# Two half-width feed-forward turns at the start of a decoder layer, with a new order of work

## The reference

```
x = x + linear_attention(layernorm(x))        # elu+1 feature map, causal sums, q k v and output projections
x = x + softmax_attention(layernorm(x), ctx)  # queries from x, keys and values from ctx, no output projection
x = x + feed_forward(layernorm(x))
feed_forward:
    h = silu((x @ w1.T) * s1) * ((x @ w2.T) * s2)     # 256 -> 1024
    h = gelu((h @ h1.T) * sh1)                        # 1024 -> 1024
    h = gelu((h @ h2.T) * sh2)                        # 1024 -> 1024
    return (h @ w3.T) * s3                            # 1024 -> 256
```

## Time and profile before

| | |
|---|---|
| median of 3 runs | 1086.01 us |
| the profiled execution | 1086.11 us, span 1084.3 us |
| PE busy | 1052.5 us, 97% of the span |
| DVE busy | 760.0 us, 70% |
| ACT busy | 554.6 us, 51% |
| POOL busy | 260.1 us, 24% |
| moved by DMA | 165.42 MB, mean 153 GB/s |

### The profile page before, as it was taken

One profiled execution on the slowest core, in us unless ns is written; L12 is line 12 of the kernel. 1 busy time (PEld: TensorE's weight loads), 2 busy tenths in 40 slices (PEclk: granted clock), 3 DMA queues, 4 the chain that ended last, 5 costly groups with the idle time before them and its releaser, 6 DMA issues.

```text
span 1084.3 us, 25055 instructions
## 1 busy us (share of the span) xinstructions
PE 1052.5 (97%) x9898; PEld 875.7 (81%) x9898; DVE 760.0 (70%) x1708; ACT 554.6 (51%) x871; POOL 260.1 (24%) x363
## 2 busy tenths in 40 slices
PE   6998899999999999999999999999999999999997
PEld 6897678787888878878878888788887888887886
DVE  5988987778777888868998767986589626423421
ACT  4344364654646455666454755465634663433431
POOL 3232351012410152011522111611027001500500
PEclk9999899999999999999999999999999999999999
DMA  4468677435633355243442325433254445555542
GB/s 132 151 207 288 212 236 240 131 106 181 195 109 132 121 190 177 79 151 116 172 148 89 118 72 187 129 117 110 100 177 123 135 136 181 187 187 171 179 156 72
DMA packets 72614, 165.42 MB, mean 153 GB/s; under 512 B 9904, under 2 KB 25392, under 8 KB 72496
## 3 DMA queue, kind: packets, MB, share of 16 engines
q1 hardware_dynamic: 69040, 152.26, 43.4%
q10 hardware_dynamic: 3456, 11.54, 3.4%
HBM read 140.66 MB, written 34.64 MB: 162 GB/s over the span
## 4 chain that ended last, share of the span: by engine, by line
PE 80%; DVE 10%; DMA 3%; issue 2%; POOL 2%; ACT 1%; SPq 1%; ACTq 0%; DVEq 0%; POOLq 0%
PE bank L1220 40%; PE bank L1105 7%; PE bank L1205 7%; PE bank L1240 5%; PE bank L1078 5%; PE bank L1047 4%; PE bank L1062 3%; PE bank L1052 2%; PE bank L1023 2%; DMA ctx_in<-in_ctxT 1%; PE bank L1155 1%; DVE mx L954 1%; DVE hidden_full L985 1%; DVE att_l L933 1%; DMA weight_ring<-weights_scratch 1%
## 5 line engine op out<-in xcount | busy, mean ns | idle before, releaser
L1220 PE MATMUL bank<-hidden_a,weight_ring 128*128 128x512 f32 x1024 | 251.9, 396 | 0.0
L1220 PE MATMUL bank<-hidden_b,weight_ring 128*128 128x512 f32 x1024 | 247.1, 394 | 0.3 <-DVE inexact_flag L1010 0.3
L1220 PEld LDWEIGHTS bank<-hidden_b,weight_ring 128*128 128x128 f32 x1024 | 188.2, 188 | 40.1 <-issue 1.2
L1220 PEld LDWEIGHTS bank<-hidden_a,weight_ring 128*128 128x128 f32 x1024 | 186.9, 188 | 39.5 <-issue 0.6
L822 ACT ACTIVATE hidden_full<-bank,columns_sb 128x512 f32<-128x512 f32 x128 | 88.2, 689 | 169.6 <-PE bank L1220 169.1
L671 POOL TENSOR_TENSOR ve<-mv,eps 128x1 f32<-128x1 f32 (+1 forms) x80 | 19.9, 249 | 491.9 <-DVE mv L837 491.9
L1205 PE MATMUL bank<-hidden_b,weight_ring 128*128 128x512 f32 x512 | 123.7, 396 | 1.3 <-DMA weight_ring<-weights_scratch 1.3
L1205 PEld LDWEIGHTS bank<-hidden_b,weight_ring 128*128 128x128 f32 x512 | 95.4, 190 | 22.5 <-DMA weight_ring<-weights_scratch 2.1
L710 POOL TENSOR_TENSOR hidden_a<-hidden_full,hidden_a 128x512 fp32r<-128x512 f32 x64 | 83.2, 1304 | 125.3 <-ACT hidden_a L817 123.8
L874 DVE STREAM_TRANSPOSE by_token<-bank 128x512 f32<-128x512 f32 x64 | 45.5, 711 | 87.7 <-PE bank L1078 87.6
L993 DVE TENSOR_TENSOR hidden_a<-hidden_full,hidden_a 128x512 fp32r<-128x512 f32 x64 | 44.0, 692 | 68.3 <-ACT hidden_a L828 68.1
(11 more groups left out here) (135 smaller groups left out, 1727.6 us busy)
## 6 DMA issues: line engine op xcount, KB each, us to landing
weight_ring<-weights_scratch SPq DMA_DIRECT2D x160, 512.0 KB, 3.7
weights_scratch<-in_h ACTq DMA_DIRECT2D x16, 512.0 KB, 5.5
xn3T_scratch<-hidden_b SPq DMA_DIRECT2D x16, 512.0 KB, 3.8
weight_bits<-in_h SPq DMA_DIRECT2D x32, 256.0 KB, 3.9
weight_ring<-weights_scratch SPq DMA_DIRECT2D x32, 256.0 KB, 2.8
x_in<-in_x SPq DMA_DIRECT2D x16, 256.0 KB, 2.8
xb<-in_x SPq DMA_DIRECT2D x16, 256.0 KB, 3.4
ctx_in<-in_ctxT SPq DMA_DIRECT2D x16, 256.0 KB, 4.4
```

The costliest lines, as they stand in the source:

```text
L1220: mm = eng.matmul(pbank(step, g, n)[:, :], ring[:, slot, kk * P:(kk + 1) * P], src[:, part, kk, :], start=(kk == 0 and part == 0), stop=(k ...
```

## The change: half-width turns for groups 0 and 1, and a new plan

Groups 0 and 1 each get a turn of their own with 256 tokens; groups 2 to 15 go two to a turn as before. There are 9 turns, and the matmuls of the first two are 128x256. Everything that was sized by turn (`res`, `HB`, `HA`, `full`, stores) takes a width `WIDE[f]`.

```diff
+    FIRST = (0, 1, *range(2, G + 1, 2))
+    TURNS = len(FIRST) - 1
+    TURN = [max(f for f in range(TURNS) if FIRST[f] <= g) for g in range(G)]
+    WIDE = [T * (FIRST[f + 1] - FIRST[f]) for f in range(TURNS)]
-    KEPT = range(1, 9)
+    KEPT = range(1, 14)
-    SPARE, PATIENCE, HOLD = 1, 5.0, 1.0
+    SPARE, PATIENCE, HOLD, MANY = 1, 8.6, 0, 2
-    PITCH = 42
+    PITCH = 49.1
+    AHEAD = 345.9, 0
+    LEAD = {("gpsimd", "bias"): -14.1, ("gpsimd", "ctx"): -18.7, ("gpsimd", "gate_rest"): 2, ("gpsimd", "ln1_stats"): -3.1,
...
-            u = 60 + 6 * g
+            u = AHEAD[0] + AHEAD[1] * g
...
-    AT = {("scalar", "split", n): (7, 7.7, 8.4, 15, 15, 15, 15)[n] for n in range(7)}
-    AT |= {("scalar", "copy_weights", j): 62 + 5.4 * j for j in range(NCH)}
+    AT = {("scalar", "split", n): (6.2, 6.9, 7.6, 9.5, 10.5, 14.5, 15)[n] for n in range(7)}
+    AT |= {("scalar", "copy_weights", j): 24 + 3.4 * j for j in range(NCH)}
...
         if step == "gate":
-            return [v("xn3T", 2 * g), v("xn3T", 2 * g + 1), d("ring", g, n // 4)]
+            return [v("xn3T", FIRST[g + 1] - 1), d("ring", g, n // 4)]
...
-    split = (wq, wk, wv, wo, xwq, xwk, xwv)
+    split = (wq, wk, wv, xwk, xwv, wo, xwq)
...
-                for dst, src, n in ((whole[0], wqT, "wq"), (whole[1], wkT, "wk"), (whole[2], wvT, "wv")):
-                    eng.dma_start(dst, src.rearrange("(c p) o -> p c o", p=P)).then_inc(weights[n], 16)
-                eng.dma_start(bvb[:, :], bv.partition_broadcast(P)).then_inc(weights["late"], 16)
-                eng.dma_start(bob[:, :], bo.partition_broadcast(P)).then_inc(weights["late"], 16)
-                eng.dma_start(xb[:, :, :], x[0:GB].rearrange("b s d -> s b d")).then_inc(xb_loaded, 16)
-                for dst, src in zip(whole[3:], (woT, xqT, xkT, xvT)):
-                    eng.dma_start(dst, src.rearrange("(c p) o -> p c o", p=P)).then_inc(weights["late"], 16)
+                for n, (dst, src) in enumerate(zip(whole, (wqT, wkT, wvT, xkT, xvT, woT, xqT))):
+                    if n == 5:
+                        load_ctx(0)
+                        eng.dma_start(bvb[:, :], bv.partition_broadcast(P)).then_inc(weights["bv"], 16)
+                        load_x(1)
+                        load_xb(0)
+                        eng.dma_start(bob[:, :], bo.partition_broadcast(P)).then_inc(weights["bo"], 16)
+                    eng.dma_start(dst, src.rearrange("(c p) o -> p c o", p=P)).then_inc(weights[SPLIT[n]], 16)
...
                         for kk in range(C):
                             at_ = ((m % 2 * 2 + z) * C + kk) * P
                             for part in range(2):
-                                mm = eng.matmul(pbank(step, g, n)[:, :], ring[:, n // 4, at_:at_ + P], HB[:, part, kk, :],
+                                mm = eng.matmul(pbank(step, g, n)[:, 0:WIDE[g]], ring[:, n // 4, at_:at_ + P], HB[:, part, kk, 0:WIDE[g]],
                                                 start=(kk == 0 and part == 0), stop=(kk == C - 1 and part == 1))
```

More of the change, by code:

```diff
@@ L140, in needs @@
     def needs(engine, step, g, n):
[L142 removed]
+        f = TURN[g] if g < G else 0
         def t(step, g, n=0): return ("tensor", step, g, n)
@@ L315, in decoder_layer_program @@
                 ff = [e for turn, e in fits if turn]
-                patient = ff and all(now - e[2][2] < PATIENCE for e in tiled) and len(tiled) < 2
+                patient = ff and all(now - e[2][2] < PATIENCE for e in tiled) and len(tiled) < MANY
                 if mode and tiled:
@@ L341, in decoder_layer_program @@
                 kind = TILED.get(step, 0)
-                if kind != mode:
-                    took += .2
+                took += CHANGE.get((mode, kind), 0)
                 mode = kind
@@ L466, in decoder_layer_program @@
             consts_loaded, cols_loaded = sem("consts_loaded"), sem("cols_loaded")
-            weights = {n: sem(f"{n}_loaded") for n in ("wq", "wk", "wv", "late")}
+            weights = {n: sem(f"{n}_loaded") for n in ("wq", "wk", "wv", "xk", "xv", "wo", "xq", "bv", "bo")}
             ln_const, const_ready, act_const, bias_ready = sem("ln_const"), sem("const_ready"), sem("act_const"), sem("bias_ready")
@@ L703, in _ @@
                         if g == 0:
-                            eng.wait_ge(weights["late"], 16 * 6)
+                            eng.wait_ge(weights["bo"], 16)
                         eng.tensor_tensor(xb[:, :, :], xb[:, :, :],
@@ L730, in _ @@
                     elif step == "split":
-                        eng.wait_ge(*((weights[("wq", "wk", "wv")[g]], 16) if g < 3 else (weights["late"], 16 * 6)))
+                        eng.wait_ge(weights[SPLIT[g]], 16)
                         eng.activation(split[g][:, 0, :, :], whole[g], ACT.Copy).then_inc(split_hi, 1)
@@ L821, in _ @@
                         wait_full(eng, g, KH + n)
-                        eng.activation(full[:, (KH + n) % NFULL, :], pbank("hidden", g, n)[:, :], ACT.Gelu, scale=sc).then_inc(h_full, 1)
+                        eng.activation(full[:, (KH + n) % NFULL, 0:WIDE[g]], pbank("hidden", g, n)[:, 0:WIDE[g]], ACT.Gelu, scale=sc).then_inc(h_full, 1)
                         if n == 0:
@@ L922, in _ @@
                             eng.wait_ge(const_ready, 5)
-                            eng.wait_ge(weights["late"], 16 * 6)
+                            eng.wait_ge(weights["bv"], 16)
                         wait_count(eng, summed[0], 4 * g)
@@ L1219, in _ @@
                             for part in range(2):
-                                mm = eng.matmul(pbank(step, g, n)[:, :], ring[:, slot, kk * P:(kk + 1) * P], src[:, part, kk, :],
+                                mm = eng.matmul(pbank(step, g, n)[:, 0:WIDE[g]], ring[:, slot, kk * P:(kk + 1) * P], src[:, part, kk, 0:WIDE[g]],
                                                 start=(kk == 0 and part == 0), stop=(kk == KH - 1 and part == 1))
@@ L1239, in _ @@
                             for part in range(2):
-                                mm = eng.matmul(pbank(step, g, c)[:, :], ring[:, slot, kk % 4 * P:(kk % 4 + 1) * P], HA[:, part, kk, :],
+                                mm = eng.matmul(pbank(step, g, c)[:, 0:WIDE[g]], ring[:, slot, kk % 4 * P:(kk % 4 + 1) * P], HA[:, part, kk, 0:WIDE[g]],
                                                 start=(kk == 0 and part == 0), stop=(kk == KH - 1 and part == 1))
```

199 lines of the change are left out of this document (112 added, 87 removed).

## The result

The changed kernel takes 1102.98 us (median of 4 runs, 1100.59 to 1107.78) against 1086.91 us for the kernel before, measured alongside: a ratio of 1.0156, 95% interval 1.0135 to 1.0176. I had forecast 1075.1 us, with 1065 to 1091 as the range. The sign was wrong. The profiled execution has a span of 1102.0 us at a mean granted clock of 0.984.

A forecast was written before the change was run, and what follows sets the result against it. PE, busy 97%, was taken as the bound, losing time to idle and lower clock, with DVE next to limit. Terms -11.4 + 0.5 - 0.7 + 0.7 = -10.9 us on 1086.11 gave 1075.2, forecast 1075.1 us, range 1065 to 1091.

The forecast's parts named there:

- The pace up to the end of the half-width turns: From 20 us on, DVE busy share 0.92 ends the half-width turns at 286.9 us, 11.4 us earlier than before.
- Narrow matmuls: In the half-width turns, 704 matmuls of 256 columns cost nothing extra; a rival with dear ones, 1098 us, had chance 0.01.
- The rest: Behind the half-width turns: 0.7 us less by 4 fewer changes between uses of PE, 0.7 us added for waits.
- the 298.3 of equal work: Time in us when the kernel before reaches the work done by the half-width turns' end; the mark to beat.
- The hole at 84 to 121: Before and in the first turn, PE's 10.1 us of idle and the slow clock behind it can go.
- DMA: From 20 to 120 us, DMA engines 93% busy, counted inside DVE's share, which would otherwise have been 0.94.
- a slower rival at 1094 us: From 20 to 300 us, full DMA engines delay value stores, ACT waits, DVE falls to 0.86; chance 0.16.
- The start: Before group 0's scores, earlier ctx weight loads and splits save 0 to 4.7 us, taken as 3, not added.
- The ring: In the half-width turns, waits for weight ring loads cost 0.5 us, between 0 and 6.
- PE's floor: Only the first wait of 8.3 us left, half-width turns end at 278.5 us; as a rival 1067 us, chance 0.2.
- The chances: Whole kernel: faster 0.73, same 0.10, slower 0.17, from cases of 0.52, 0.2, 0.11, 0.16 and 0.01.
- the third: Rival for the whole kernel: no change, 1086 us within 0.3%, PE's holes only move; chance 0.11.

The follow-up runs named there:

- split_in_two: Kernel before, each of the 2,816 feed-forward matmuls of 512 columns issued as two of 256 with the same weights: 1114.58 us, ratio 1.0249.
- whole_turns: Changed kernel with the turns put back to eight of full width, new plan and initial loads kept: 1093.73 us, ratio 1.0078.
- half_ring_took: Changed kernel with first four ring loads planned from 105 us on and planner's kept-key load duration 8.5 instead of 5 us: 1094.64 us, ratio 1.0067.
- half_took: Changed kernel with only the planner's duration for a load of kept keys raised from 5 to 8.5 us: 1095.12 us, ratio 1.0062.
- whole_took: Changed kernel with eight whole turns and the planner's duration for a load of kept keys raised from 5 to 8.5 us: 1086.10 us, ratio 0.9997.
- loads_only: Kernel before with only the new initial loads, order of weight splits and their readiness rules; whole turns, old plan constants: 1092.52 us, ratio 1.0057.
- split_128: Kernel before with feed-forward matmuls issued as two halves, each cut to its first 128 columns: 1167.95 and 1224.49 us in two executions.

## Why the prediction was wrong

The profiled execution took 1103.85 us, 28.7 more than the 1075.2 of my sum. The half-width turns ended at 300.2 us where I had 286.9, which is 13.3 of it; behind them I had 0.7 us for waits and the runs show 15.7, which is 15.0 more. Three steps failed.

*The pace up to the end of the half-width turns: wrong.* My -11.4 us rests on "I take 0.92" for DVE's busy share, "since PE must be full at once". DVE ran at 0.863 from 20 to 300 us (241.51 of 280), and PE wasn't full: it was idle 22.4 us up to the end of the half-width turns (300.4 less 277.98), where the kernel before was idle 20.4 us up to the end of its first turn (252.4 less 231.96). The hole of 84 to 121 went, and one at 50 to 57 came. The gain I counted on was PE's idle time, and in sum none of it went.

*Narrow matmuls: wrong.* "704 x 0.1135 = 79.9 us, as 352 x 0.227" is the step that failed for the half-width turns. I took the pitch from one row of 12 matmuls in the attention; in the feed-forward's stream it is 0.12 us. By split_in_two this is 352 x 0.010 = 3.5 us. The windows say nearly the same. These two count only the feed-forward's matmuls, in whole_turns up to the end of its first turn and in the changed kernel up to the end of the second half-width turn:

```profile
0.00:296.60 296.60, 90.33 (x352) 0.98 0.58 184
0.00:300.40 300.40, 94.52 (x705) 0.98 0.68 220
```

So they cost 4.2 us of PE's busy time. The 9.1 us in my expectation for half_ring_took (95.2 against 86.1) compared with the mean of all eight turns, most of which run with less attention in between, and it matched the 9 us between whole kernels by luck. The rest of those 9 us isn't all spent in the half-width turns either. The last feed-forward matmuls of the changed kernel and of whole_turns end 10.7 us apart (1095.4 and 1084.7), but those of the turn for groups 2 and 3, the next after the narrow ones, only 3.4 us (434.9 and 431.5); the other 7.3 us come where both have turns of equal width. In half_took and whole_took it is 8.0 of 8.8 us by that turn. The Trainium skill, in "TensorE: Matmul & The Clock Gate", section "Back-to-back issue gap", spoke against my step, and I gave it 0.01. Its direction held, its sizes didn't: measured are 0.11, 0.119 and 0.227 us at 128, 256 and 512 columns, where it has 0.081 and 0.131 at 128 and 512.

*The rest: wrong, and the largest in size.* The line "I add 0.7 us for waits" for everything behind 300 us. The half-width turns ended 1.9 us behind the 298.3 of equal work, but the last `w3` matmuls 17.6 us late, so some 15.7 us were lost behind 300. I read the order there only by its counts of instructions and changes of mode, and never looked how far each consumer stands behind its load. half_took shows that the planner's duration for the key loads made 13.5 us of it in the two profiled executions, about half as waits and half as work at the lower clock; between the whole kernels it is 7.9 us by the medians and 10.2 by the ratios. The condition I had written, new waits over 5 us behind 300 us, came true in sum (12.3 us); none alone is over 2.7 us.

*The hole at 84 to 121: right, and of no use.* PE was busy 6.8 us more there. The same happens with whole turns (33.33 us in whole_turns) and doesn't with the old plan (27.43 in loads_only), so it is the new plan that does it. One group less to wait for moved the first turn by 3.7 us.

*DMA: right mechanism, wrong place and size.* I forecast 93% busy from 20 to 120 us, and it was 85%, with a store of values that holds up ACT, as a slower rival at 1094 us with DVE at 0.86. ACT waited 15.6 us for stores, over my limit of 10, in six waits, of which one, at 50 to 57 us, has 8.8. Taking that one away gave 0.5 to 1.9 us in three pairs. DVE's 0.863 is close to that rival's share, and its work by then was 253.7 us against my 255.0. But from 150 us on PE was busy 148.31 of 150 us, so there DVE waited for PE and not the other way round.

*The start: right.* 4.4 us, within my 0 to 4.7. In loads_only, where the rest of the order came out otherwise too, it was worth nothing at the end.

*The ring: right within its bounds.* 2.5 us of waits against 0.5, with 6 as the upper end.

*PE's floor: wrong.* At 278.5 us it was too low by the dearer matmuls, and PE's idle time was not only the first wait of 8.3 us: up to 300 us PE was busy 277.6 and idle 22.4, and part of its work ran at the lower clock (0.92 from 42 to 84 us).

*The chances* don't add up as I wrote them: 0.52 and 0.2, with 0.02 of the third, make 0.74 for faster and not 0.73, and with 0.02 more to the other side 0.19 for slower and 0.07 for the same.

What stays open: why kernels with the half-width turns are 9 to 10 us slower in three plans and 4.4 to 6.9 in a fourth (7.1 to 9.2 and 3.9 to 5.8 by the ratios), when 4.2 us of it are the narrow matmuls' busy time. Each pair also differs in the order of everything behind the first turns, and no run holds that order still. Open too is what sets the 0.119 us, the weight load or something beside it.

## What to carry to other kernels

Price a split instruction by a long run of its own kind, and see whether the weight loads still have room: at 81% busy with 512 columns they went to 93% with halves. Compare it with the same turn of the other kernel, and not with the mean of all turns. In an order that a planner writes, look for each load at how far its consumer stands behind it and compare that with issue, queue and landing in the trace; one understated duration cost some 8 to 10 us, and one number mended it. Count with each wait the work behind it that runs at the lower clock. And when each new order moves the time by several microseconds either way, a gain of 4 us at the start proves nothing until the end is measured; take turns, plan and loads apart before you believe in any of them.

## What the runs showed of the hardware

- A matmul of 128 columns with a weight load of its own follows the next by 0.11 us at full clock, hardly faster than 256 columns at 0.119, and by 0.214 us at 1.2 GHz.
- Behind waits of PE of 2.3 to 2.7 us at 483, 613 and 742 us the same 32 scores took 2.09 us instead of 1.17, at a granted clock of 0.50 (1.2 GHz). In half_took, without these waits, PE was busy 6.9 us less for the same number of matmuls (775.68 against 782.58 us).
- In the profiled execution of split_128 the granted clock was 0.62 from 900 to 1000 us and 0.50 (1.2 GHz) from 1000 to 1100, while PE was busy 99 and 100 of 100 us; what it did before and then was little but matmuls of 128 columns, each with its weight load. split_in_two, with 256 columns, had 0.99 from 900 to 1082 us. One execution shows this, and no run tells the cause.
- One store of 512 KB took about 13 us to land behind four ring loads and beside the copies, with a median of 6.2 us.
